# A shorter page front, later first norms, and an even rate of row adds in the third feed-forward layer

## The reference

```
x = x + 0.5 * ffn0(layernorm(x))     # layer 0: 8 experts, top 2, width 176, and a shared part
x = x + attn0(layernorm(x))          # the kernel's "mixing"
x = x + 0.5 * ffn0(layernorm(x))     # layer 1: the same weights again
x = x + 0.5 * ffn1(layernorm(x))     # layer 2: 32 experts, top 6, width 96, and a shared part
x = x + attn1(layernorm(x))          # linear attention with rotary keys and queries
x = x + 0.5 * ffn1(layernorm(x))     # layer 3
```

```
QKV = X @ W_in.T + b_in;  Q = rope(Q);  K = rope(K)
A = sum over rows of (K / |K|) * V
Y = (A * Q) @ W_out.T + b_out;   return Y + X
```

## Time and profile before

| what | value |
|---|---|
| median of 3 runs | 1301.58 us (1299.71 to 1303.45) |
| the profiled execution | 1301.21 us |
| its span, first to last instruction | 1299.4 us |
| PE busy | 1110.7 us (85%) |
| DVE busy | 746.4 us (57%) |
| POOL busy | 594.8 us (46%) |
| ACT busy | 536.0 us (41%) |
| mean granted TensorE clock | 0.929 |

### The profile page before, as it was taken

One profiled execution on the slowest core, in us unless ns is written; L12 is line 12 of the kernel. 1 busy time (PEld: TensorE's weight loads), 2 busy tenths in 40 slices (PEclk: granted clock), 3 DMA queues, 4 the chain that ended last, 5 costly groups with the idle time before them and its releaser, 6 DMA issues. The chain is left out here.

```text
span 1299.4 us, 20577 instructions
## 1 busy us (share of the span) xinstructions
PE 1110.7 (85%) x6035; PEld 918.2 (71%) x6035; DVE 746.4 (57%) x2345; ACT 536.0 (41%) x1012; POOL 594.8 (46%) x579
## 2 busy tenths in 40 slices
PE   4899997887898999988687899999968674899994
PEld 3777775566677887766565799988545553899994
DVE  4663365645635574366645564777788655545554
ACT  3423344464533432244441344444242324466663
POOL 3580244221213233237767303667536777017776
PEclk9799998999988999999888999999888887899998
DMA  9623535920000236534353767887302232569997
GB/s 315 281 94 90 154 102 166 323 98 1 1 1 33 87 141 257 201 120 144 127 198 129 234 209 218 282 252 226 92 8 81 102 106 101 176 205 285 295 288 239
DMA packets 126073, 209.84 MB, mean 161 GB/s; under 512 B 16064, under 2 KB 105536, under 8 KB 124096
## 3 DMA queue, kind: packets, MB, share of 16 engines
q1 hardware_dynamic: 101392, 141.38, 32.8%
q0 software_dynamic: 24576, 67.14, 16.6%
HBM read 129.29 MB, written 101.19 MB: 177 GB/s over the span
## 5 line engine op out<-in xcount | busy, mean ns | idle before, releaser
L713 POOL DMA_INDIRECT G<-yd,slot_of x256 | 251.1, 981 | 297.9 <-DMA yd<-yo 216.4
L698 POOL DMA_INDIRECT xd<-xnt,slot_of x256 | 251.6, 983 | 152.4 <-issue 78.7
L982 PE MATMUL ps<-WE,xT 128*128 x1016 | 190.0, 331 | 0.6 <-issue 0.2
L2210 DVE TENSOR_TENSOR hid<-hid,ps 128x192 f32<-128x192 f32 (+2 forms) x168 | 65.3, 389 | 180.9 <-ACT hid L1624 180.6
L982 PEld LDWEIGHTS ps<-WE,xT 128*128 128x128 f32 x1016 | 164.7, 193 | 2.7 <-issue 2.6
L2189 DVE SCALAR_TENSOR_TENSOR XT<-G,wt,XT 128x256 f32<-128x256 f32 x256 | 127.6, 503 | 62.1 <-DMA G<-yd,slot_of 52.9
L1595 ACT ACTIVATE xT<-ps 128x512 f32<-128x512 f32 (+1 forms) x168 | 99.0, 589 | 140.4 <-PE ps L949 134.6
L1624 ACT ACTIVATE hid<-ps 128x192 f32<-128x192 f32 (+2 forms) x168 | 60.3, 359 | 164.3 <-PE ps L982 164.3
L949 PE MATMUL ps<-ident,xd_in 128*128 128x128 f32 x664 | 102.5, 276 | 29.7 <-DMA xd_in<-xd 20.7
L949 PEld LDWEIGHTS ps<-ident,xd_in 128*128 128x128 f32 x664 | 81.5, 142 | 42.9 <-issue 23.3
L1452 ACT ACTIVATE S<-ps 128x512 f32<-128x512 f32 (+1 forms) x72 | 42.6, 592 | 159.7 <-PE ps L887 157.4
(11 more groups left out here) (265 smaller groups left out, 2168.4 us busy)
## 6 DMA issues: line engine op xcount, KB each, us to landing
xd_in<-xd SPq DMA_DIRECT2D x140, 256.0 KB
yd<-yo SPq DMA_DIRECT2D x140, 256.0 KB, 3.2
WE<-w SPq DMA_DIRECT2D x8, 1280.0 KB, 10.2
xd_in<-xd SPq DMA_DIRECT2D x52, 128.0 KB, 2.3
yd<-yo SPq DMA_DIRECT2D x52, 128.0 KB, 2.0
W0E<-w0e SPq DMA_DIRECT2D x1, 4864.0 KB, 33.3
xd<-xnt,slot_of POOLq DMA_INDIRECT x256, 2.4
G<-yd,slot_of POOLq DMA_INDIRECT x256, 4.1
```

What stands on the lines that cost most here:

```text
L698: nc.gpsimd.indirect_dma_start(xd[f // 2][:, :], bass.IndirectOffsetOnAxis(ap=slot_of[:, t, k:k + 1], axis=0), xnt[:, t, :], None).then_in ...
L713: nc.gpsimd.indirect_dma_start(G[:, n % G_RING, :], None, yd[f // 2][0:min(ly.upto[t][k], ly.TILES) * P, :], bass.IndirectOffsetOnAxis(ap= ...
L982: last = mm(dst, xT[:, q % 2, a, k, :], flat[:, bass.ds(expert[2 * q + a] + k * 2 * ly.H, 2 * ly.H)], start=(k == 0), stop=(k == KD - 1))
L2210: tt(hid[:, q % 2, 0:m, 0:ly.H], hid[:, q % 2, 0:m, 0:ly.H], src, ALU.mult).then_inc(TL.hid, 1)
```

## The change

`FRONT` of layer 2 goes from 16 to 12, so that SyncE waits for all scatters before pair 6 and not before pair 8, `MOVED` goes from 24 to 22, and the first gathers may go when 22 pairs are sent. The tables of `attn1` are fetched behind the pages of pair 12 and not behind those of pair 3. VectorE adds two gathered rows in each pair (before: two, and a third in each fourth pair), from the same pair 29 on. The first two norms of `attn1` start later in the run, further from each other, and the third one's statistics move from pair 62 into the window. Its root is taken by ScalarE and its reciprocal by VectorE, no longer by GpSimd. In the window VectorE's remaining row adds (26 and not 17) stand at other places.

```diff
-FRONT = [0, 0, 16, 0]
+FRONT = [0, 0, 12, 0]
...
             def attention_weights(i):
-                if i == 3:
+                if i == 12:
...
             for t in range(TT):
                 gather(2, t)
-                if t in (4, 8, 12):
-                    inverse(AT_NORM, (t - 4) // 4)
+                if t in (5, 9):
+                    inverse(AT_NORM, (t - 5) // 4)
...
             def first_turns(i):          # TensorE
-                if i == 47:
+                if i == 50:
                     turn(AT_NORM, 0, xnt, B_BANK)
-                if i == 57:
+                if i == 61:
                     pe.wait_ge(AT_NORM.hi, 1)
                     turn(AT_NORM, 1, xnt, B_BANK)
...
             def first_turns(i):          # ScalarE
-                if i == 43:
+                if i == 47:
                     rows(AT_NORM, 0, XT[:, tiles_of(0), :])
-                if i == 49:
+                if i == 52:
                     flipped(0, B_BANK)
-                if i == 54:
-                    rows(AT_NORM, 1, XT[:, tiles_of(1), :])
                 if i == 59:
+                    rows(AT_NORM, 1, XT[:, tiles_of(1), :])
+                if i == 63:
                     flipped(1, B_BANK)
...
             def window():                # ScalarE
-                rows(AT_NORM, 2, XT[:, tiles_of(2), :])
                 keys(0)
+                std(AT_NORM, 2)
+                rows(AT_NORM, 2, XT[:, tiles_of(2), :])
...
-                    for _ in range(per_pair + (1 if FRONT[f] and (q - q0) % 4 == 3 else 0)):
+                    for _ in range(per_pair):
...
             def first_turns(i):          # VectorE
-                if i in (40, 51, 62):
-                    b = (i - 40) // 11
+                if i in (41, 53):
+                    b = (i - 41) // 12
                     dve.wait_ge(g_used, GATHER0[2] + (b + 1) * NG)
                     stats(AT_NORM, b, XT[:, tiles_of(b), :])
-                if i in (42, 53, 63):
-                    offsets(AT_NORM, (i - 42) // 10)
+                if i in (46, 58):
+                    offsets(AT_NORM, (i - 46) // 12)
                 if i == 50:
                     dve.wait_ge(att_in, 16 * 6)
                     residual(0)
-                if i == 58:
+                if i == 61:
                     residual(1)
...
                 rotated(0, "k1", KB[:, 0, 0, :], A1.krot)      # VectorE's window
-                gathers(2)
+                gathers(3 * NG - m[0])
+                dve.wait_ge(g_used, GATHER0[2] + 3 * NG)
+                stats(AT_NORM, 2, XT[:, tiles_of(2), :])
                 key_values(0)
                 key_inverse(0)
+                gathers(2)
+                offsets(AT_NORM, 2, True)
                 rotated(0, "q1", QT[:, 0, 0, :], A1.qrot)
                 key_sums(0)
-                gathers(2)
+                gathers(4)
                 rotated(1, "k1", KB[:, 1, 0, :], A1.krot)
-                gathers(4)
+                gathers(6)
                 key_values(1)
                 key_inverse(1)
-                gathers(4 * NG - m[0])
+                gathers(4)
                 rotated(1, "q1", QT[:, 1, 0, :], A1.qrot)
                 key_sums(1)
                 weighted()
+                gathers(4 * NG - m[0])
                 last_stats()
...
-            m = tiles(2, 2, 5, first_turns)
+            m = tiles(2, 2, 7, first_turns)
```

More of the change, by code:

```diff
@@ L1773, in first_turns @@
             def first_turns(i):
-                if i == 43:
+                if i == 47:
                     rows(AT_NORM, 0, XT[:, tiles_of(0), :])
-                if i == 49:
+                if i == 52:
                     flipped(0, B_BANK)
-                if i == 54:
+                if i == 59:
                     rows(AT_NORM, 1, XT[:, tiles_of(1), :])
-                if i == 59:
+                if i == 63:
                     flipped(1, B_BANK)
@@ L1832, in window @@
                 chunks = [ch for b in range(NB) for ch in RUN["s", 3, b][0]]
+                keys(0)
+                std(AT_NORM, 2)
                 rows(AT_NORM, 2, XT[:, tiles_of(2), :])
-                keys(0)
                 key_rows(1)
```

## The result

The changed kernel takes 1304.35 us (median of 20 runs) where the kernel before has 1300.08: ratio 1.0037 with a 95% interval of 1.0024 to 1.0051. I had forecast 1295.3 and a range to 1302.5. The profiled execution has a span of 1303.1 us against 1299.4.

| stretch, us | before | after | measured | predicted |
|---|---|---|---|---|
| before layer 2's run (no edit touches it) | 712.12 | 710.38 | -1.7 | 0 |
| first turned pages to pair 8 | 28.1 | 31.3 | +3.2 | +3.9 |
| pair 8 to pair 45 (tables at pair 12) | 104.6 | 108.3 | +3.7 | +1.0 |
| pair 45 to pair 63 | 59.7 | 52.6 | -7.1 | -6.6 |
| pair 63 to the first key matmul | 9.5 | 7.05 | -2.5 | -3.4 |

The account below looks back on a forecast made before the run. TensorE was taken to bound most of layer 2's run and VectorE the window behind it; +3.9 + 1.0 - 6.6 - 3.4 - 0.8 = -5.9 us took 1301.2 to 1295.3, range 1290 to 1302.5.

Parts of the forecast that it names:

- The start: Layer 2's run up to pair 8: longer TensorE idle and half clock, scatters ending 3.47 us sooner; loss of 3.9 us.
- rival (b): Start of the run: front too short and scatters end no sooner, pair 8 loses 7.3 us; kernel 1298.7, chance 0.10.
- The tables at pair 12: Pair 13's pages queue behind the tables' 3.7 us of issue time; stall taken as 1.0 us, range 0 to 4.8.
- the two landings that I had weighed: Pair 13's page landing: 2.7 us gives no stall, pair 4's 8.07 us gives a stall of 4.8 us.
- Rival (a): Tables stall pair 13 in full, 4.8 us and not 1.0, and hold up results; kernel 1299.1, chance 0.13.
- The second half and the run's end: Pair 45 to the first key matmul: stalls shrink to 0.5 us (-6.6), last wait and slow clock go (-3.4).
- rival (e): Second half: stalls only move to pairs 50, 53 and 61, 4 of the 6.6 us stay; kernel 1299.3, chance 0.08.
- the two grounds that I gave: Second half: two adds a pair fit GpSimd's gather rate; GpSimd's roots stand one tile later, so it no longer waits.
- The window: Run's end to layer 3's first statistics, bounded by VectorE: 8.1 us added, 8.9 gone, -0.8; bounds -4.6 to +9.3.
- Rival (d): Window: ScalarE's root comes in time (-2.4), block 2's residual falls beside other work (-1.9); kernel 1291.0, chance 0.11.
- I count one add held up and not two (-1.9): Window: GpSimd's block 2 residual, starting when VectorE is at the query rotation, holds up one add; 1.9 us gained.
- Rival (c): Window pays in full, +9.3 us for adds, statistics, offset and root wait; kernel 1305.4, chance 0.13.

Follow-up runs that it names:

- e4: Changed kernel with the attention tables fetched at pair 24 and not at pair 12; 1302.73 us, ratio 1.0027.
- e7: Changed kernel with the extra add at every fourth pair put back, so 79 adds in the run and 17 in the window; 1300.02 us, ratio 1.0008.
- e5: Changed kernel with GpSimd's two residual adds of blocks 2 and 3 cut to 8 columns; 1293.57 us, ratio 0.9963.
- e12: Kernel before with GpSimd's residual adds of blocks 2 and 3 cut to 8 columns; 1293.71 us, ratio 0.9975.
- e8: Changed kernel with 16 front pages, tables at pair 24, root ahead of query copy, residuals between gathers and behind layer 3's second norm; 1285.58 us, ratio 0.9885.
- e1: Kernel before with only the front of 12 pages and the tables at pair 12; 1304.81 us, ratio 1.0039.
- e3: Changed kernel with GpSimd adding the residuals of blocks 2 and 3 only after VectorE has written WSH; 1301.39 us, ratio 1.0014.
- e2: Changed kernel with the front of 16 pages and the tables at pair 3 as before; 1295.73 us, ratio 0.9985.

## Why the prediction was wrong

**The start** was right in mechanism and near in size: GpSimd's waits of 1.91 and 2.16 us are gone, so rival (b) falls, pair 6 is turned at 733.60 behind 7.99 us of idle and is followed by half clock, and pair 8 comes 3.2 us later (predicted 3.9). Some of that is luck: pair 6 came 1.4 us sooner than summed, and the clock took 0.8 us more. That the two waits are transfers taking turns, as I wrote, the trace does not show; it shows them only together with the tables.

**The tables at pair 12** were sized too small: 3.7 us and not 1.0. Pair 13 was issued at 750.89 and turned 6.5 us later (757.39), between the two landings that I had weighed, so the stall itself is 1.6 us. The other 2.1 are the pair behind it, which takes 4.95 us and not 2.83, a loss that I had counted behind the long wait and not behind the short one. Rival (a) had 4.8 and is the nearer; e4 shows that the whole 3.7 goes with the tables. A landing of 6.5 us against the 2.7 of a pair alone fits a pair that queues behind the tables. The Trainium skill (DMA: Bandwidth & Descriptors, Queues, rings and completion order) has each transfer engine take the descriptors of a ring in their order; that agrees, and no run separates it from other causes.

**The second half and the run's end** were right in size: -7.1 and -2.5 against -6.6 and -3.4. H is 59.66 or 59.67 us in every kernel with 70 adds in the run and the norms' new places, so rival (e) falls. Of the two grounds that I gave, the rate of adds carried little: e7 has the old rate and loses 1.4 us.

**The window** is the step that failed: -0.8 predicted, +7.4 measured. Rival (d), that it hides what it is given, falls with that. The sum of work and waits was nearly right: leaving hold-ups aside it makes +1.0 (8.1 less 1.7, 1.5, 3.3 and 0.55), and e5 against e12 shows +1.8. The step that failed is "I count one add held up and not two (-1.9)". I had read from the earlier trace rows that a residual holds up adds, and took it that VectorE's work at the new place would slip past. Measured up to the first statistics, hold-ups and half clock cost 6.3 us (50.13 - 43.79) against 4.4 before (46.40 - 41.95): +1.9 and not -1.9. Held-up operations alone went from 3.8 to 4.3 us, for the residual fell on the 128x2 operation and `WSH` and did not slip past them; the rest is half clock, of which 1 us is chance. And my sum ended at layer 3's first statistics, while the earlier trace rows ask for the first scatter: between first and second statistics block 3's residual costs 2.9 us, where before the change VectorE was still waiting for the projection. By the gain of 3.3 us that I booked for these waits, I had uncovered it; in e7, where they are back (0.77 and 1.77 us), the same residual costs 1.0 us. Another 1.05 us goes behind them, where a turn of TensorE runs at half clock (1.94 us and not 1.07). So 1.8 + 1.9 + 2.7 + 1.05 = 7.45. My lower bound of -4.6 was also mis-added: its terms (-0.8 - 2.4 - 1.9) make -5.1.

The Trainium skill's rule (SBUF — State Buffer, SBUF: two separate sides) speaks of VectorE operations with two SBUF inputs and also of those in a mode that uses both ports. I had used the first half only, for the sum, and let it stand beside the forecast at +1.6. The rows agree as far as they go: the one-input `TENSOR_SCALAR` on `WOUT` and on 128x4 numbers waited as well, though no row shows in which mode it ran, and operations with an operand in PSUM, the statistics and the `RECIPROCAL` did not. Rival (c), the window in full, came nearest to the time (1305.4), and for the wrong reason: its deciding point, 51.5 us to the first statistics, was not reached (50.13), and gathers never ran short in the window. Two of my own signs did show it: more than 50 us to those statistics, if barely, and a first scatter of layer 3 at 983.74 where I had 975.

## What to carry to other kernels

When GpSimd adds or multiplies in SBUF, price its whole duration against VectorE's additions and multiplications in SBUF at that time, small ones included (here the statistics, the `RECIPROCAL` and work with a PSUM operand kept their time), and follow the sum to the point where the next stage really starts. Put such an operation where VectorE reads PSUM or waits for TensorE; e8 does so with one of two residuals, and that one costs nothing. A wait that you remove may have been the cover of another engine's work. Two stages that help and hurt should be built apart: here the changed kernel's order of the run, with 16 pages in front again and with GpSimd's work, the root and the tables moved, is 1.15% faster than before (e8).

## What was not expected of the hardware

How long VectorE is held up does not depend on the size of its operation: 128x2 numbers took 2.36 us beside a GpSimd operation of 2.35, against 0.16 alone. It works the other way too, weakly: GpSimd's addition took 2.69 and not 2.34 us beside VectorE's sum of two SBUF operands in e8. TensorE lost 2.1 us in the pair behind a stall of only 1.42 us, at a granted clock of 0.50. The kernel before waits 1.41 us at pair 8, keeps a clock of 1.00 there and loses nothing; e1 lost 2.3 us behind a wait of 1.06, and e5 0.4 behind 0.85. What decides it is open. Why the same wait of 3.1 us was followed by 6.65 and 6.49 us for eight query matmuls in two executions (the changed kernel, e3) and by 5.23 to 5.41 in three others (e2, e4, e5) is open.
